# Order of the experts' products, fillers and the last recurrent sums in a fused two-layer decoder kernel

## What is computed

```python
# mixture of experts: E = 8, two experts a token, cap = 512 rows an expert, hidden 512
logits = xt @ wg; gates_k, idx_k = top_k(softmax(logits), 2)
loc = running count of earlier rows with the same expert
disp[idx_k, loc] += xt * (loc < cap)
h   = relu(einsum('ecd,edh->ech', disp, w1) + b1)     # first product of each expert
out = einsum('ech,ehd->ecd', h, w2) + b2              # second product
y   = sum over both choices of gate * out[idx_k, loc]

# linear attention with decay
v = x @ W_write.T
reads = (mask * decay * (x @ x_shifted.T)) @ v        # chunks of 64 positions
x = layernorm(x + x + alpha * reads @ W_read.T)

# recurrence over the positions t of a sequence, k = x, v = ctx
A_t = exp(-w) * A + exp(k) * v;  B_t = exp(w) * B + exp(-k)
out = A + exp(u + k) * (v * B + max(t - 1, 0))

# last block: the 7 best of 64 tokens of each sequence by x @ router_w go through
# attention and a feed-forward part, the others are passed on
```

## Time and profile before

| | |
|---|---|
| runs shown | 427.66, 430.13 and 428.51 us, median 428.51 us |
| profiled execution | 427.36 us, span 425.6 us |
| busy share of the span | TensorE 85%, weight loads 60%, VectorE 58%, ScalarE 48%, GpSimd 45% |
| TensorE's granted clock, mean | 0.933 of 2.4 GHz |
| self and cross attention, with norms and feed-forward | to about 184 us |
| routing, up to the first gathered rows | 184 to 209 us |
| experts, up to the last scatter | 209 to 302 us |
| read back, linear attention, recurrence, choice of tokens | 302 to 389 us |
| last block and output | 389 to 425.6 us |

### The profile page before, as it was taken

The page is one execution under the profiler, slowest core; times in us unless marked ns, Lnnn a source line. Parts: engine busy times, 40 slices in busy tenths (PEclk is TensorE's granted clock), DMA queues, the critical chain, the costliest instruction groups (busy, mean ns, idle before and its releaser), DMA issues.

```text
span 425.6 us, 8220 instructions
## 1 busy us (share of the span) xinstructions
PE 360.7 (85%) x3220; PEld 255.6 (60%) x3220; DVE 247.7 (58%) x734; ACT 202.5 (48%) x359; POOL 191.7 (45%) x235
## 2 busy tenths in 40 slices
PE   5999999999989999984577677889968898989880
PEld 2677775666767777852254355567445675677560
DVE  1788994689999689688300000001279989546531
ACT  1677785744478867455423322333155544214630
POOL 3244546854442131140765556664235545691113
PEclk9999999999999999998588898999989999866995
DMA  8999700000000000011120111110430000010000
GB/s 282 415 406 399 243 4 2 2 0 2 2 0 4 2 2 2 2 51 49 43 57 31 43 37 45 43 43 32 134 91 0 2 0 1 26 51 25 2 2 13
DMA packets 18361, 27.54 MB, mean 65 GB/s; under 512 B 2418, under 2 KB 13683, under 8 KB 17683
## 3 DMA queue, kind: packets, MB, share of 16 engines
q1 hardware_dynamic: 15682, 22.43, 14.8%
q0 software_dynamic: 2112, 4.33, 3.5%
q10 hardware_dynamic: 528, 0.26, 0.2%
HBM read 20.59 MB, written 6.42 MB: 63 GB/s over the span
## 4 chain that ended last, share of the span: by engine, by line
PE 56%; DVE 17%; ACT 8%; another core or an unknown queue 5%; POOL 4%; issue 4%; DMA 3%; POOLq 0%; SPq 0%; DVEq 0%; ACTq 0%
PE bank L1040 8%; PE bank L448 7%; PE bank L425 7%; PE bank L435 7%; PE bank L1047 4%; PE bank L912 3%; PE bank L863 2%; PE bank L591 2%; DVE x_tok L559 2%; DVE stats L1786 2%; PE bank L408 2%; ACT hT L1423 1%; POOL rstd L582 1%; DMA q_diag<-in_q_self 1%
## 5 line engine op out<-in xcount | busy, mean ns | idle before, releaser
L398 POOL TENSOR_TENSOR scratch<-k_comp,con 128x512 f32<-128x512 f32 x34 | 35.6, 1048 | 50.7 <-PE bank L425 36.6
L508 DVE TENSOR_REDUCE neg_max<-bank 128x16 f32<-128x1024 f32 x34 | 41.6, 1223 | 23.0 <-PE bank L425 22.9
L591 PE MATMUL bank<-mask_bf,ident_bf 128*128 128x512 bf16 x181 | 48.3, 401 | 3.8 <-DVE mask_bf L1540 3.4
L1768 DVE TENSOR_TENSOR probsT<-bank,mb 128x512 f32<-128x512 f32 x7 | 4.8, 692 | 77.3 <-remote 51.4
L480 ACT COPY probsT<-bank 128x1024 f32<-128x1024 f32 x34 | 34.4, 1013 | 26.6 <-PE bank L435 26.5
L1040 PE MATMUL bank<-probs,mw 128*128 128x512 f32 x64 | 36.7, 726 | 11.4 <-ACT probs L1416 9.1
L751 POOL DMA_INDIRECT choice_rows<-probsT,place x32 | 31.3, 978 | 28.1 <-DVE probsT L1768 20.0
L448 PEld LDWEIGHTS bank<-v_pair,probsT 128*64 128x64 f32 x1088 | 34.6, 138 | 14.0 <-issue 9.6
L581 POOL TENSOR_SCALAR var_e<-mv 128x4 f32<-128x4 f32 x28 | 9.4, 337 | 74.2 <-DVE mv L1590 38.1
L491 ACT ACTIVATE probs<-probs 128x1024 f32<-128x1024 f32 x34 | 35.9, 1055 | 13.3 <-DVE probs L535 13.3
L448 PE MATMUL bank<-v_pair,probsT 128*64 128x18 f32 x1088 | 37.9, 212 | 3.3 <-ACT probsT L480 3.2
(11 more groups left out here) (294 smaller groups left out, 685.4 us busy)
## 6 DMA issues: line engine op xcount, KB each, us to landing
mw<-in_mw SPq DMA_DIRECT2D x2, 2048.0 KB, 14.9
v_pair<-in_v_self SPq DMA_DIRECT2D x4, 576.0 KB, 10.6
q_diag<-in_q_self SPq DMA_DIRECT2D x4, 512.0 KB, 9.7
choice_rows<-hT SPq DMA_DIRECT2D x1, 2048.0 KB
con<-in_const SPq DMA_DIRECT2D x1, 1249.5 KB, 14.3
k_comp<-in_k_self SPq DMA_DIRECT2D x4, 256.0 KB, 8.8
x_tok<-in_x SPq DMA_DIRECT2D x1, 1024.0 KB, 10.3
ctxT<-in_ctxT SPq DMA_DIRECT2D x1, 1024.0 KB, 9.7
```

The lines of the kernel that those rows point to most:

```text
L398: mult(k_heads[:, i % 2], k_comp[:, i, :, None, :].to_broadcast([P, 2, HG, S]), hm, ALU.mult).then_inc(s["spread"], 1)
L508: have_m = link.mark(nc.vector.tensor_reduce(m, sc, AX, ALU.max, negate=True))
L591: nc.tensor.matmul(bank[:, bk, :], ident_bf[:, :], mask_bf[:, 0, None, :].to_broadcast([P, 8, S]), start=True, stop=True)
```

## The change

TensorE: the two products of the combined weights move ahead of the ranks and right behind them; 14 fillers instead of 16 before the slot search; 36 fillers instead of 4 ahead of the first turn. The experts' order becomes hidden(0), turn_in(1), hidden(1), output(0), hidden(2), output(1), ..., output(6), hidden(7), output(7), and five fillers stand ahead of each turn inside an `output`. In the skewed loop the turn of ln7 quad 2 moves from the end of round 4 to round 5, behind the sums of quad 3; the third rows are gathered ahead of the last `weights`; `gather_facts(1)` moves behind it; fillers of 4, 3 and 2 are added. ScalarE: its copies follow the same order; those of the weights move up. VectorE: `between` moves behind three more operations. GpSimd and SyncE are unchanged.

```diff
@@ -1003,13 +1003,17 @@
             residuals(3)
             project_out(3)
 
+            pe.wait_ge(s_r["logits"], 3)
+            tr(bank[:, 3, 0:P], wcomb[:, P:2 * P], ident).then_inc(s_lin["w"], 1)
             keep(6, 16)
             pe.wait_ge(s_r["chosen"], 1)
             steps = bank[:, 0, 0:256].rearrange("p (e n) -> p e n", e=E)
             oh = chosen_bf[:, :, :].rearrange("p n e -> p e n")
             mm(steps, earlier_bf, oh, start=True, stop=False)
             mm(steps[:, :, 1:], later_bf, oh[:, :, 0:TOPK * NT - 1], start=False, stop=True).then_inc(s_r["ranks"], 1)
-            keep(2, 16)
+            pe.wait_ge(s_lin["w_sb"], 1)
+            mm(bank[:, 2, 0:P], wcomb[:, 0:P], wcomb[:, 2 * P:3 * P], start=True, stop=True).then_inc(s_lin["w"], 1)
+            keep(6, 14)
 
             for n in range(TOPK * NT):
                 if n % 8 == 0:
@@ -1019,11 +1023,6 @@
                 last = mm(bank[:, 4, 0:E * 2 * CT], rank_hot[:, n], slot_hot[:, n].rearrange("p e c -> p (e c)"),
                           start=n == 0, stop=n == TOPK * NT - 1)
             last.then_inc(s_r["found"], 1)
-
-            tr(bank[:, 3, 0:P], wcomb[:, P:2 * P], ident).then_inc(s_lin["w"], 1)
-            pe.wait_ge(s_lin["w_sb"], 1)
-            mm(bank[:, 2, 0:P], wcomb[:, 0:P], wcomb[:, 2 * P:3 * P], start=True, stop=True).then_inc(s_lin["w"], 1)
-            pe.wait_ge(s_lin["w_sb"], 2)
 
             def turn_in(e):
                 pe.wait_ge(s_moe_in[e], 16 * CT)
@@ -1047,20 +1046,27 @@
                         last = mm(cols4(out_bank(j), j), hT[:, v % 2, f, j * P:(j + 1) * P], mw2[:, v, f],
                                   start=f == 0, stop=f == FC - 1)
                     if j == 2 and next_in:
+                        keep(6 + next_in % 2, 5)
                         turn_in(next_in)
                     if v == E - 1:
                         last.then_inc(s_mo, 1)
                 if v < E - 1:
                     last.then_inc(s_mo, 1)
 
-            keep(5, 4)
+            pe.wait_ge(s_lin["w_sb"], 2)
+            keep(5, 36)
             turn_in(0)
-            for e in range(E - 1):
+            hidden(0)
+            turn_in(1)
+            for e in range(1, E - 1):
                 hidden(e)
-                if e >= 2:
-                    pe.wait_ge(s_moe["out"], e - 1)
-                output(e, lambda j: 4 + e % 2, e + 1)
+                if e >= 3:
+                    pe.wait_ge(s_moe["out"], e - 2)
+                output(e - 1, lambda j: 4 + (e - 1) % 2, e + 1)
+            pe.wait_ge(s_moe["out"], E - 3)
+            output(E - 2, lambda j: 4 + (E - 2) % 2)
             hidden(E - 1)
+            keep(6, 4)
             pe.wait_ge(s_moe["out"], E - 1)
             output(E - 1, lambda j: LAST_BANKS[j])
             keep(3, 40)
@@ -1180,6 +1186,7 @@
                 if w >= NQ:
                     spread_places(w - NQ)
                 if w == NQ + 1:
+                    ln_pe(pe, ln["ln7"], 2, x_tok)
                     weights(2)
                 if w < NQ:
                     scores_values(w)
@@ -1187,6 +1194,8 @@
                     ln_pe(pe, ln["ln6"], w - 1, x_tok, fill=1)
                 if w < NQ:
                     reads(w)
+                if w == NQ:
+                    keep(1, 4)
                 if w in (3, 4):
                     weights(w - 3)
                 if w == NQ:
@@ -1195,11 +1204,13 @@
                     gather_mask(0)
                     gather_rows(1)
                     spread_places(2)
-                    gather_facts(1)
-                if w >= 2:
+                    keep(1, 3)
+                if w in (2, 3, 5):
                     ln_pe(pe, ln["ln7"], w - 2, x_tok, fill=2 if w < NQ else 0)
+            gather_rows(2)
             weights(3)
-            gather_rows(2)
+            keep(6, 2)
+            gather_facts(1)
             spread_places(3)
             gather_facts(2)
             gather_mask(1)
@@ -1383,7 +1394,11 @@
             norm_act("ln4", 1)
             act.wait_ge(s_r["logits"], NQ)
             cp(tiles22(work[:, NT - 4:NT]), projection(NQ - 1)[:, :, :, 0:P]).then_inc(s_oTs, 1)
+            act.wait_ge(s_lin["w"], 1)
+            cp(wcomb[:, 2 * P:3 * P], bank[:, 3, 0:P]).then_inc(s_lin["w_sb"], 1)
             norm_act("ln4", 2)
+            act.wait_ge(s_lin["w"], 2)
+            cp(wcomb[:, 3 * P:4 * P], bank[:, 2, 0:P]).then_inc(s_lin["w_sb"], 1)
 
             act.wait_ge(s_r["rows"], 1)
             for n in range(16, 24):
@@ -1404,10 +1419,6 @@
             link(A(col("log_gamma"), col("t2"), ACT.Ln))
             link(nc.scalar.mul(col("log_gamma"), col("log_gamma"), -1.0))
             A(decay[:, :], con_at("decay_steps"), ACT.Exp, scale=col("log_gamma")).then_inc(s_lin["consts"], 1)
-            act.wait_ge(s_lin["w"], 1)
-            cp(wcomb[:, 2 * P:3 * P], bank[:, 3, 0:P]).then_inc(s_lin["w_sb"], 1)
-            act.wait_ge(s_lin["w"], 2)
-            cp(wcomb[:, 3 * P:4 * P], bank[:, 2, 0:P]).then_inc(s_lin["w_sb"], 1)
 
             def input_out(e):
                 act.wait_ge(s_moe["turned"], e + 1)
@@ -1462,6 +1473,8 @@
                 if q >= 0:
                     act.wait_ge(s_rec["tok"], q + 1)
                     cp(work[:, 4 * q:4 * q + 4].rearrange("p t d -> p (t d)"), bank[:, 6]).then_inc(s_rec["taken"], 1)
+                if w == NQ + 1:
+                    ln_act(act, ln["ln7"], 2)
                 q = w
                 if q < NQ:
                     act.wait_ge(s_lin["v"], q + 1)
@@ -1480,11 +1493,14 @@
                     A(seqs(rec_b(q, 2))[:, :, 2:S], seqs(k)[:, :, 1:S - 1], ACT.Exp, scale=-1.0).then_inc(s_rec["scan"], 1)
                     A(rec_b(q, 0), k, ACT.Exp).then_inc(s_rec["exp_k"], 1)
                     A(rec_b(q, 3), k, ACT.Exp, bias=col("u")).then_inc(s_rec["exp"], 1)
-                if w >= NQ:
-                    half_out(w - NQ)
+                if w == NQ:
+                    half_out(0)
                 if w >= 2:
                     norm_act("ln7", w - 2)
-                    ln_act(act, ln["ln7"], w - 2)
+                    if w != NQ:
+                        ln_act(act, ln["ln7"], w - 2)
+                if w == NQ + 1:
+                    half_out(1)
             half_out(2)
             act.wait_ge(s_sel["gathered"], 2 * NQ - 1)
             cp(hT_flat[:, 256:512], bank[:, 0, 0:NS * P]).then_inc(s_slot["act"], 1)
@@ -1833,13 +1849,13 @@
                     dve.wait_ge(s_rec["tok"], q - 1)
                 dve.wait_ge(s_rec["scan"], q + 1)
                 n = link.mark(nc.vector.tensor_tensor_scan(bb, eg, rec_b(q, 2), 0.0, ALU.mult, ALU.add))
-                if between:
-                    between()
                 dve.wait_ge(s_rec["exp_k"], q + 1)
                 keys = link.mark(tt(seqs(rec_b(q, 1))[:, :, 2:S], seqs(rec_b(q, 0))[:, :, 1:S - 1], seqs(c)[:, :, 1:S - 1], ALU.mult))
                 link.wait(n)
                 link(tt(bb, bb, c, ALU.mult))
                 link(tt(bb, bb, con_at("steps"), ALU.add))
+                if between:
+                    between()
                 dve.wait_ge(s_rec["exp"], q + 1)
                 tt(bb, bb, rec_b(q, 3), ALU.mult).then_inc(s_rec["mult"], 1)
                 link.wait(keys)
```

## The result

The changed kernel takes 0.9941 of the time before (95% interval 0.9913 to 0.9969; 20 runs of each, medians 429.13 and 430.13 us). That is about 2.5 us faster, where 10 were forecast. All ratios here compare fast runs alone and the medians take in every run, among them two of the changed kernel with 528.22 and 531.21 us. The profiled execution takes 423.19 us with a span of 421.3, 4.3 under that of before; it is the fastest of the twenty, so its own 4.3 overstate the gain.

The account below looks back on a forecast made before the run. It took GpSimd and TensorE waiting on each other in 12.4 us laps, with results seen late, plus half clock, to bound the experts' stage. 427.36 - 8.5 - 1.5 = 417.4, with 1.15 for the median 418.5 us; range 410 to 430.5.

Parts of the forecast that it names:

- Part 1: Start: earlier weights' products and 36 fillers before the first turn; net 0 us (bounds -2 to +5.4), first result about 226.3.
- Part 2: Experts' laps: second products behind the next first product give slack; last scatter 293.5, -8.5 us (bounds -13 and 0).
- the ends move into the scatter half, where the trace has only first products, and none of them late: Experts: with TensorE at 9 us and GpSimd at 10.2, second products end during scatters, so results are not late.
- stays busy: Experts: GpSimd's results come a first product later in TensorE's order, but TensorE keeps working at full clock.
- Two late laps of four: Experts: two laps of 12.4 us and two of 10.2 us, last scatter at 293.5, -8.5 us.
- the 0.85 us saved per expert pays for the fillers: Experts, TensorE: lap 9.0 us against 8.6 undisturbed before, so the order alone buys nothing there.
- Part 3: Recurrences and tail: moved shift, earlier last sums, later gathers and fillers; -1.5 us in all (bounds -7 and +4).
- the moved shift: Second and third recurrences: VectorE's later `between` delays TensorE's norms, up to 2 us each; 1 each taken, +2 us.
- the rest: Recurrences and tail: last sums ahead of quad 2's turn -2 us, later gathers -1, tail clock -0.5.
- Laps always late: Rival, experts: results still released only behind the gathers; experts -2 us, tail -1.5, 425 us; chance 0.25.
- the moved norm holds TensorE: Rival, turns of quads 0 and 1: 2.1 us each, +4.2, last sums return nothing; 432 us; chance 0.18.
- The signs: Right: first product under 4 us, two laps of 10 to 11, last scatter near 292. Wrong: TensorE idle over 2 us.

Follow-up runs that it names:

- the two first parts alone: Kernel before with only the early weights' products, 36 start fillers, staggered second products and five fillers per turn; recurrences and tail as before: 0.9930, 3.0 us less.
- the kernel with the norm back: Changed kernel with VectorE's `between` back directly behind the recurrence's first scan in all three recurrences that have it: ratio 0.9844 to the kernel before.
- the run with the recurrence part: Kernel before with only earlier last sums, moved gathers, recurrence fillers and VectorE's later shift; experts and routing as before: 0.9962, 1.6 us less.
- the decisive pair: Changed kernel with SyncE storing results by plain transfers, plus four unread gathers per late expert: 422.94 us (0.9840); with pauses of two GpSimd additions behind each four transfers: 419.67 us (0.9741).

## Why the prediction was wrong

- **Part 1** held: the 36 fillers take 9.54 us (forecast 10.0), the first product 3.70, and the first result is seen at 227.0 (226.3).
- **Part 2** failed. It forecast 8.5 us and a last scatter at 293.5; the scatter ends at 301.07, and the two first parts alone gave 3.0 us. The step that failed is "the ends move into the scatter half, where the trace has only first products, and none of them late". They did not move. TensorE's ends of the second to fifth result stand at 235.46, 245.94, 262.32 and 274.67: in GpSimd's sixth, sixth and eighth transfer and 0.2 us behind the eighth. The prediction's own numbers put the first of them there (226.3 + 9.0 is 7.4 us into a lap that begins at 227.9). The later ones were to drift out, with TensorE at 9.0 us a lap, since it "stays busy". But the turn of the next rows is held back as well, TensorE stands idle for it (6.06 us in one lap), and each late lap sets the old phase again.
- Nor is the scatter half safe. Transposes that ended during the fourth scatter were seen 7.3 us late, and in the kernel whose rows come by SyncE nine scatters alone hold results back. The prediction took the kind of transfer, or the half of the lap, for the cause; the runs show that it is GpSimd's unbroken issuing of either kind, with the reservation made above. A result that comes just as a run ends makes GpSimd go on almost without a gap, and the next is the later for it: the gain of one lap is taken back in the next (10.9, then 13.0 us). "Two late laps of four" was a middle without a row.
- The step "the 0.85 us saved per expert pays for the fillers" was wrong as a trade: without the fillers in the laps the kernel with the norm back is 3.7 us faster by the ratios (0.9844 and 0.9759, whose intervals overlap) and 3.8 by the traces.
- **Part 3** came out as a sum (0.9962, 1.6 us; forecast 1.5), but by luck, and its interval reaches no change. Two terms were both too small and cancel: the moved shift costs 3.7 us, not 2, and the rest returns 5.0 to 6.9, not 3.5. The prediction took the shift's price for up to 2 us in each of two rounds and halved it without a row; the trace has nearly all of it in the first.
- **The rivals.** "Laps always late" is the case that came (425 forecast; 0.9941 of 428.51 is 426.0), with part of "the moved norm holds TensorE" in it. It had 0.25. Its row, four laps of 12.4 us whatever the clock did, should have weighed more than the argument against it, though the run with the recurrence part shows that the same experts' part can also have a lap of 10.2 us.
- **The signs.** Right: the first product is under 4 us, no fillers run behind 212, and the last sums are 2.4 us nearer to the end (368.88 of 421.3). Wrong: only one of four laps is under 11 us, the last scatter is issued at 300.10, the clock is at half from 248.3 to 255.1 and from 265.3 to 268.8, and TensorE idles 2.69 us at quad 0.

## What to carry to other kernels

Where one engine's finished work is seen late, look at what another engine issues meanwhile, and price a reordering by the pattern of late rows until an experiment has its cause. Ask whether what holds a result back also holds the engine that makes it: if it does, the phase between the two does not drift as their free-running laps would have it. Fillers that keep the clock up cost their full time where the engine is on the path. Test each part of an edit alone: here the version with the shift moved in the fourth recurrence only and without fillers in the laps gains nearly five times what the whole change did.

## What the runs showed of the hardware

- While GpSimd issues indirect transfers (128 rows of 512 bytes, 1.25 to 1.28 us apart) without a break, what TensorE finishes late in the run is seen by the others mostly only behind its end: up to 2.3 us behind a run of eight, 2.0 to 3.4 behind most of sixteen to twenty, 5.1 behind 32. Early in a run it is on time, or nearly: up to the tenth transfer of the first run of sixteen (0.2 us late in both kernels of the decisive pair), and up to the fourth of a later one (0.03 us in the changed kernel with the norm back, 0.9 at most elsewhere) if a break stood ahead of it. A gap of 1.0 us (changed kernel) or 1.3 us (one addition) did not count as a break; 2.4 us did. In runs of four with such gaps all was on time. In the run of 32 TensorE's own passes came 0.7 to 2.8 us apart.
- "SBUF — State Buffer" of the Trainium skill, section "SBUF: two separate sides", excludes a slowdown of engines by transfers at the ports. The 3.70 us of a first product beside gathers agree with it, so the signals' delay has another way, which no run here shows. That it is GpSimd's issuing and not the moved bytes is supported by SyncE's transfers: the same bytes issued there held nothing back. Plain transfers issued by GpSimd were not tried.
- The granted clock of the tail, 375 us and on, fell to half for 10 us and more in some executions of kernels with the same tail and not in others. From the last sums to the end it took 52.1 us in the changed kernel with the norm back, where the clock stayed full, and 56.4 in the same kernel with 4 fillers at the start, where it was at half from 375 to 385 us.
